# ScalarE takes over one search round of one of VectorE's tiles in three groups of the second step

## The reference

```python
def _adj_from_feats(Xa, W1, W2, W3):
    logits = (Xa @ W1) @ W2 @ (Xa @ W3).T
    idx = jnp.argsort(-logits, axis=1)
    csum = jnp.cumsum(softmax(take_along_axis(logits, idx, 1)), axis=1)
    k_i = jnp.sum(csum < 0.9, axis=1) + 1       # how many of the largest make up 0.9 of the mass
    keep = the k_i largest of each row
    return softmax(where(keep, logits, -inf))

for s in range(2):
    A = _adj_from_feats(Xa, W1, W2, W3)
    Xf = Rf @ Xf;  Xb = Rb @ Xb;  Xa = A @ Xa   # Rf, Rb: adj scaled by its row and column sums
    Z = Z + (Xf @ U1[s] + Xb @ U2[s] + Xa @ U3[s])
```

## Time and profile before

| | |
|---|---|
| median of 3 runs | 3602.8 us (3601.22 to 3603.57) |
| the profiled execution's own time | 3600.57 us |
| its span, first to last instruction | 3598.8 us |
| VectorE, ScalarE, TensorE busy | 95%, 85%, 80% of the span |
| step 1, group 0 begins on VectorE | at 1587.8 us of the span |
| step 1, VectorE takes over role 1 | at 3008.9 us |

### The profile page before, as it was taken

One profiled execution on the slowest core, in us unless ns is written; L12 is line 12 of the kernel. 1 busy time (PEld: TensorE's weight loads), 2 busy tenths in 40 slices (PEclk: granted clock), 3 DMA queues, 4 the chain that ended last, 5 costly groups with the idle time before them and its releaser, 6 DMA issues. The chain is left out here.

```text
span 3598.8 us, 40441 instructions
## 1 busy us (share of the span) xinstructions
PE 2864.5 (80%) x13536; PEld 2020.1 (56%) x13536; DVE 3434.2 (95%) x4607; ACT 3074.2 (85%) x4185; POOL 467.9 (13%) x483
## 2 busy tenths in 40 slices
PE   6568787878778787646888888879797973789998
PEld 5456566666657576422454454536353552657787
DVE  7999999999999999969999999999999998788997
ACT  6999999999999999759999999999999994455443
POOL 3000000000000000000000000000000000546676
PEclk9679898999889898878998999989898996999999
DMA  2112221223121221054221112111121210578996
GB/s 97 58 67 75 71 91 64 88 69 100 55 98 59 89 71 51 22 161 100 48 50 33 47 41 55 31 50 41 42 47 40 52 18 21 163 198 236 252 266 175
DMA packets 224256, 305.43 MB, mean 85 GB/s; under 512 B 81328, under 2 KB 160624, under 8 KB 220656
## 3 DMA queue, kind: packets, MB, share of 16 engines
q1 hardware_dynamic: 187648, 223.01, 21.5%
q10 hardware_dynamic: 21744, 62.79, 5.0%
q0 software_dynamic: 14656, 17.04, 3.3%
HBM read 232.80 MB, written 59.77 MB: 81 GB/s over the span
## 5 line engine op out<-in xcount | busy, mean ns | idle before, releaser
L738 DVE SCALAR_TENSOR_TENSOR s_dump<-s_rows,s_mid 128x3328 bf16<-128x3328 f32 x551 | 2027.1, 3679 | 1.6 <-issue 0.6
L691 ACT ACTIVATE s_adump<-s_rows,s_mid 128x3327 int8<-128x3327 f32 x295 | 906.0, 3071 | 9.5
L697 ACT ACTIVATE s_adump<-s_rows,s_mid 128x3327 int8<-128x3327 f32 x295 | 902.4, 3059 | 0.0
L952 PE MATMUL bank<-x,s_slab 128*128 128x512 f32 x1352 | 630.5, 609 | 0.0
L952 PEld LDWEIGHTS bank<-x,s_slab 128*128 128x128 f32 x1352 | 264.6, 197 | 277.7 <-issue 265.7
L929 PE MATMUL bank<-kh,qs 128*128 128x512 f16 (+1 forms) x364 | 144.7, 398 | 345.5 <-DVE s_rows L717 324.9
L996 PE MATMUL bank<-hb,s_wT 128*128 128x256 f32 x1352 | 353.4, 406 | 66.5 <-ACT s_wT L570 66.1
L996 PE MATMUL bank<-xab,last_wT 128*128 128x256 f32 x1300 | 337.3, 404 | 50.3 <-ACT last_wT L570 50.2
L952 PE MATMUL bank<-hb,s_slab 128*128 128x257 f32 x1352 | 351.7, 401 | 0.0
L985 PE MATMUL bank<-ident,s_rows 128*128 128x128 f32 x1222 | 206.4, 296 | 153.9 <-DVE s_rows L793 153.0
L996 PEld LDWEIGHTS bank<-hb,s_wT 128*128 128x128 f32 x1352 | 258.8, 202 | 115.2 <-ACT s_wT L570 51.5
(11 more groups left out here) (217 smaller groups left out, 5127.0 us busy)
## 6 DMA issues: line engine op xcount, KB each, us to landing
s_slab<-adjT_dram SPq DMA_DIRECT2D x104, 448.0 KB, 3.7
s_slab<-adjT_dram SPq DMA_DIRECT2D x104, 384.0 KB, 3.6
e_adj<-adjR_dram ACTq DMA_DIRECT2D x23, 1664.0 KB, 7.5
strip<-adjR_dram SPq DMA_DIRECT2D x52, 448.0 KB, 3.5
strip<-adjR_dram SPq DMA_DIRECT2D x52, 384.0 KB, 3.2
e_ring<-sc_d SPq DMA_DIRECT2D x72, 256.0 KB, 3.7
sc_d<-e_stage SPq DMA_DIRECT2D x60, 256.0 KB, 2.6
su_d<-s_su_out ACTq DMA_DIRECT2D x26, 256.0 KB, 2.0
```

Source lines behind the costliest of these rows:

```text
L691: nc.scalar.activation(adump[:], row(g, r), ACT.Sign, bias=st(mid, g, 2), accum_out=cnt[:]).then_inc(S["a_eval"], 1)
L697: nc.scalar.activation(adump[:], row(g, r), ACT.Abs, bias=st(mid, g, 2), accum_out=gap[:]).then_inc(S["a_eval"], 1)
L738: nc.vector.scalar_tensor_tensor(out=dump[:], in0=wide_row(g, r), scalar=st(mid, g, r), in1=wide_row(g, r), op0=ALU.is_le, op1=ALU.mult, a ...
L952: ins = nc.tensor.matmul(acc, slab[:, i % NSLAB, j - PIECES[p], :], s_op[:, j, 0:SN], start=False, stop=(j == NT - 1))
```

## The change

In step 1, for the groups in `HANDED` = (2, 4, 6), ScalarE does the first round (number 0) of role 0, a tile of VectorE's, after its own 19 rounds of the group before, and leaves the new `mid` where VectorE reads it. It takes `begin` for it too, with its own scale, and the last factor -1 turns the sign of ScalarE's `mid` into VectorE's. VectorE leaves out that round's `evaluate`, `judge` and `move` and half of `begin`, and at its round 1 of role 0 waits for ScalarE's semaphore `a_mid`. The counts of all semaphores are changed to suit (`passes`, `handed_to`, `opened`).

For this `sides`, `above` and the two passes are written as functions `signs`, `spread`, `distances`, `settle`. In all of ScalarE's rounds, of both steps, the instruction that computes `mean` moves: it stood before the second pass, behind `fac`, and now stands between `sgn` and the new `mid`.

```diff
+    HANDED = (2, 4, 6) if s == 1 else ()
+
+    def handed_to(g):
+        return sum(h <= g for h in HANDED)
+
+    def passes(g, it, r):
+        return BISECT * g + it - (handed_to(g if it else g - 1) if r == 0 else 0)
...
-            def begin(g, r):
+            def begin(n, g, r, own):
...
-            def sides(g, it):
+            def signs(g, r, own):
+                nc.scalar.activation(adump[:], row(g, r), ACT.Sign, bias=st(mid, g, own), accum_out=cnt[:]).then_inc(S["a_eval"], 1)
+
+            def distances(g, r, own, n):
+                act.wait_ge(S["a_eval"], 2 * n + 1)
+                nc.scalar.activation(over[:], cnt[:], ACT.Identity, scale=st(mid, g, own), bias=st(target, g, own)).then_inc(S["a_over"], 1)
+                nc.scalar.activation(adump[:], row(g, r), ACT.Abs, bias=st(mid, g, own), accum_out=gap[:]).then_inc(S["a_eval"], 1)
+
+            def spread(g, it, own, last):
                 up, down = rate(it)
-                last = -1.0 if it + 1 == BISECT else 1.0
-                nc.scalar.activation(fac[:], st(mid, g, 2), ACT.Copy, scale=last * (down - up) / 2).then_inc(S["a_fac"], 1)
-                nc.scalar.activation(mean[:], st(mid, g, 2), ACT.Copy, scale=last * (down + up) / 2).then_inc(S["a_fac"], 1)
...
+                nc.scalar.activation(fac[:], st(mid, g, own), ACT.Copy, scale=last * (down - up) / 2).then_inc(S["a_fac"], 1)
...
                 nc.scalar.activation(sgn[:], gap[:], ACT.Sign, scale=-1.0, bias=over[:]).then_inc(S["a_sgn"], 1)
+                nc.scalar.activation(mean[:], st(mid, g, own), ACT.Copy, scale=last * (down + up) / 2).then_inc(S["a_fac"], 1)
                 act.wait_ge(S["a_sgn"], n + 1)
                 act.wait_ge(S["a_fac"], 2 * n + 2)
-                nc.scalar.activation(st(mid, g, 2), sgn[:], ACT.Identity, scale=fac[:], bias=mean[:]).then_inc(S["a_mid"], 1)
+                nc.scalar.activation(st(mid, g, own), sgn[:], ACT.Identity, scale=fac[:], bias=mean[:]).then_inc(S["a_mid"], 1)
...
-                    settle(g, n)
+                    settle(g, it, 2, n, last)
+                if g + 1 in HANDED:
+                    n = BISECT * (g + 1) + handed_to(g)
+                    begin(g + 1 + handed_to(g), g + 1, 0, 0)
+                    signs(g + 1, 0, 0)
+                    spread(g + 1, 0, 0, -1.0)
+                    distances(g + 1, 0, 0, n)
+                    settle(g + 1, 0, 0, n, -1.0)
...
             def evaluate(g, it, r):
-                n = BISECT * g + it
-                if it == 0:
-                    dve.wait_ge(begun[r], 2 * (g + 1))
+                if r == 0 and g in HANDED and it == 1:
+                    dve.wait_ge(begun[0], opened(g, 0))
+                    dve.wait_ge(S["a_mid"], BISECT * g + handed_to(g))
+                elif it == 0:
+                    dve.wait_ge(begun[r], opened(g, r))
                 else:
-                    dve.wait_ge(mid_ready[r], n)
-                if n + r >= 1:
-                    dve.wait_ge(mass_done[1 - r], n + r)
+                    dve.wait_ge(mid_ready[r], passes(g, it, r))
+                other = passes(g, it + r, 1 - r)
+                if other >= 1:
+                    dve.wait_ge(mass_done[1 - r], other)
...
-                        evaluate(g, it, r)
-                        if it + r >= 1:
+                        first = 1 if g in HANDED else 0
+                        if 2 * it + r >= first:
+                            evaluate(g, it, r)
+                        if 2 * it + r > first:
                             move(g, it + r - 1, 1 - r)
                         between(g, 2 * it + r)
-                        judge(g, it, r)
+                        if 2 * it + r >= first:
+                            judge(g, it, r)
```

More of the change, by code:

```diff
@@ L538, in exponent, with settle @@
                                      accum_out=st(Z, g, r)).then_inc(S["exp_done"], 1)
-            def begin(g, r):
+            def begin(n, g, r, own):
                 act.wait_ge(S["exp_done"], LOADS.index((g, r)) + 1)
-                nc.scalar.activation(st(target, g, 2), st(Z, g, r), ACT.Copy, scale=2.0 * P_NUC - 1.0).then_inc(S["a_begun"], 1)
-                nc.scalar.activation(st(mid, g, 2), st(Z, g, r), ACT.Copy, scale=-LEAST * 2.0 ** LOG_STEP).then_inc(S["a_begun"], 1)
-                act.wait_ge(S["a_begun"], 2 * (g + 1))
-            def sides(g, it):
-                up, down = rate(it)
-                last = -1.0 if it + 1 == BISECT else 1.0
-                nc.scalar.activation(fac[:], st(mid, g, 2), ACT.Copy, scale=last * (down - up) / 2).then_inc(S["a_fac"], 1)
-                nc.scalar.activation(mean[:], st(mid, g, 2), ACT.Copy, scale=last * (down + up) / 2).then_inc(S["a_fac"], 1)
[L552 to L556, removed]
+                nc.scalar.activation(st(target, g, own), st(Z, g, r), ACT.Copy, scale=2.0 * P_NUC - 1.0).then_inc(S["a_begun"], 1)
+                nc.scalar.activation(st(mid, g, own), st(Z, g, r), ACT.Copy, scale=-LEAST * 2.0 ** LOG_STEP).then_inc(S["a_begun"], 1)
+                act.wait_ge(S["a_begun"], 2 * (n + 1))
+            def signs(g, r, own):
[5 more added lines that the diff above has]
+            def spread(g, it, own, last):
+                up, down = rate(it)
+                nc.scalar.activation(fac[:], st(mid, g, own), ACT.Copy, scale=last * (down - up) / 2).then_inc(S["a_fac"], 1)
+            def settle(g, it, own, n, last):
+                up, down = rate(it)
                 act.wait_ge(S["a_over"], n + 1)
@@ L687, in _ @@
                 r, rounds = (1, FIRST_PART) if g == LAST else (2, BISECT)
-                begin(g, r)
+                begin(g + handed_to(g), g, r, 2)
                 for it in range(rounds):
-                    n = BISECT * g + it
-                    nc.scalar.activation(adump[:], row(g, r), ACT.Sign, bias=st(mid, g, 2), accum_out=cnt[:]).then_inc(S["a_eval"], 1)
-                    sides(g, it)
+                    n = BISECT * g + it + handed_to(g)
+                    last = -1.0 if it + 1 == BISECT else 1.0
+                    signs(g, r, 2)
+                    spread(g, it, 2, last)
                     for b in beats(g, 2 * it):
                         fill(g, b)
-                    above(g, n)
-                    act.wait_ge(S["a_eval"], 2 * n + 1)
-                    nc.scalar.activation(adump[:], row(g, r), ACT.Abs, bias=st(mid, g, 2), accum_out=gap[:]).then_inc(S["a_eval"], 1)
+                    distances(g, r, 2, n)
                     for b in beats(g, 2 * it + 1):
                         fill(g, b)
-                    settle(g, n)
+                    settle(g, it, 2, n, last)
[6 more added lines that the diff above has]
+                    settle(g + 1, 0, 0, n, -1.0)
             for b in range(2 * FIRST_PART + NGRP + 4, 2 * BISECT):
@@ L753, in alone @@
             def alone(it):
-                n = BISECT * LAST + it
                 if it == 0:
-                    dve.wait_ge(begun[0], 2 * (LAST + 1))
-                    dve.wait_ge(mass_done[1], n)
+                    dve.wait_ge(begun[0], opened(LAST, 0))
+                    dve.wait_ge(mass_done[1], passes(LAST, 0, 1))
                 else:
-                    dve.wait_ge(mid_ready[0], n)
+                    dve.wait_ge(mid_ready[0], passes(LAST, it, 0))
                 nc.vector.scalar_tensor_tensor(out=dump[:], in0=wide_row(LAST, 0), scalar=st(mid, LAST, 0), in1=wide_row(LAST, 0),
@@ L774, in go_on @@
                     dve.wait_ge(begun[1], 2 * LAST + 1)
-                    dve.wait_ge(mass_done[0], BISECT * TRIPLES)
+                    dve.wait_ge(mass_done[0], passes(LAST, BISECT, 0))
                 dve.wait_ge(mid_ready[1], n + 1)
@@ L791, in cut @@
                 else:
-                    dve.wait_ge(mid_ready[r], BISECT * (g + 1))
+                    dve.wait_ge(mid_ready[r], passes(g, BISECT, r))
                 nc.vector.scalar_tensor_tensor(out=wide_row(g, r), in0=wide_row(g, r), scalar=st(mid, g, r), in1=wide_row(g, r),
```

16 lines of the change are left out of this document (8 added, 8 removed).

## The result

The changed kernel takes 3625.2 us (median of 4 runs) against 3602.0 us of the kernel before (4 runs, those shown ahead among them): ratio 1.0067, 95% interval 1.0056 to 1.0079, so 23 us slower. The profiled execution has a span of 3623.8 us.

The account below looks back on a forecast made before the run. ScalarE's group start, TensorE's gapless stretch and VectorE's eleventh take were taken as the bound. Delays of 8.6, 18.0 and 25.9 us in groups 2, 4 and 6, plus 0.1 from step 0, gave 3602.8 + 26.0 = 3628.8 us; range 3612 to 3636.

Parts of the forecast that it names:

- The chain: Inside a group: ScalarE's start, some 80 us of TensorE without a gap, VectorE's eleventh take, then VectorE's own work.
- the takes of groups 2, 4 and 6: VectorE's waits for TensorE's logits: some 38 us of new waits in these groups and not elsewhere.
- The price of a handed round: Each round added to ScalarE ahead of groups 2, 4 and 6: 7.94 us, three times, 23.8 us.
- The moved `mean`: In ScalarE's rounds: nothing with a bank between passes, +0.09 us in the others, 0.7 us a group (bounds 0 and 1.7).
- The delays: Lateness per group against the kernel before, passed from ScalarE's starts to VectorE's eleventh takes, +26.0 us at the end.
- VectorE's eleventh takes: VectorE's eleventh `take` of logits in a group; room 0.0 us in groups 2 and 4, 1.0 in 3, 1.5 in 6.
- ScalarE's waits: For TensorE's transposes, group 2 to the take-over: 25.2 us before, to stay above 20 us.
- TensorE's solid stretch too: TensorE's gapless work after ScalarE's group start, 80.7 of 80.7 us busy in group 2, starts 8.6 us late there.
- the first wait of group 8: ScalarE's 4.3 us wait for VectorE's cut, which was forecast 2.8 us nearer, so the wait shrinks by that.
- The second rival (the waits fill up): ScalarE's waits absorb the added work as TensorE gets ahead: about 0, 3603 us; half filled, +13; chance 0.10.
- VectorE as the bound: Rival: VectorE, busy 95%, sets the time and the handed rounds are free: -12.1 us, 3590.7 us; chance 0.03.
- The take-over as the place of the loss: Rival: takes don't hold VectorE, only ScalarE's end does, where VectorE takes over: +20.6 us, 3623 us; chance 0.12.

Follow-up runs that it names:

- e3: Kernel before plus ScalarE's three extra rounds, written to an unread scratch, and the moved `mean`; VectorE keeps all its own rounds: 3626.1 us against 3601.9.
- e4: Kernel before with VectorE's first role 0 round left out in groups 2, 4 and 6, done by nobody; ScalarE as before: 3599.1 us against 3601.9.
- e6: The whole change with TensorE's sweeps respread in groups 1 to 7 of step 1 (9 halves, not 14, in beats 3 to 21): 3609.7 us against 3602.1.
- e7: Handed rounds in groups 2, 4 and 6, `mean` in its old place, sweeps spread as in e6: 3603.0 us against 3602.1 for the kernel before.
- e2: The change with `mean` put back in its old place, so only the handed rounds: 3619.5 us against 3601.9 for the kernel before.
- e12: Only groups 3 and 6 handed, `mean` in its old place, sweeps as in e6, logits one beat earlier in those groups: 3594.9 us against 3601.7 before.
- e1: The change without handed rounds, so only `mean` moved: 3604.9 us against 3601.9 for the kernel before.

## Why the prediction was right, point by point

Forecast were 3628.8 us and +26.0, measured 3625.2 us and +23.2.

**The chain.** Right, and shown from four sides: the lateness of ScalarE alone gives the whole loss (e3), less work on VectorE alone gives next to nothing (e4), TensorE's work in between carries it (e6 and e7 against the change and e2), and where both are loosened, with two handed rounds, the saving comes out (e12). The waits stand where they were said to: at the takes of groups 2, 4 and 6, 33.2 us in place of "some 38".

**The price of a handed round.** Right: 7.94 us forecast, and ScalarE's timeline has its `begin` for group 2's handed round at 1921.87 and the next at 1929.82, 7.95 us.

**The moved `mean`.** Mis-sized: it was forecast at half of what it cost. A round with nothing between the passes, after the change:

```profile
2412.61 3.07 ACT L554 ACTIVATE s_adump<-last_row,s_mid 128x3327 int8<-128x3327 f32 x1
2415.59 0.19 ACT L554 ACTIVATION_READ_ACCUMULATOR s_adump<-last_row,s_mid 128x1 f32 x1
2415.68 0.19 ACT L563 ACTIVATE s_fac<-s_mid 128x1 f32<-128x1 f32 x1
2415.80 0.39 ACT L558 ACTIVATE s_over<-s_cnt,s_target,s_mid 128x1 f32<-128x1 f32 x1
2416.10 3.06 ACT L559 ACTIVATE s_adump<-last_row,s_mid 128x3327 int8<-128x3327 f32 x1
2419.06 0.19 ACT L559 ACTIVATION_READ_ACCUMULATOR s_adump<-last_row,s_mid 128x1 f32 x1
2419.34 0.29 ACT L569 ACTIVATE s_sgn<-s_gap,s_over 128x1 f32<-128x1 f32 x1
2419.54 0.19 ACT L570 ACTIVATE s_mean<-s_mid 128x1 f32<-128x1 f32 x1
2419.82 0.39 ACT L573 ACTIVATE s_mid<-s_sgn,s_mean,s_fac 128x1 f32<-128x1 f32 x1
2420.24 3.07 ACT L554 ACTIVATE s_adump<-last_row,s_mid 128x3327 int8<-128x3327 f32 x1
```

The new `mid` starts 0.48 us after `sgn`, not 0.42: it follows the start of `mean` by 0.28 us, not by its 0.19 and 0.03. In front, `over` comes 0.21 us after the reading out, not 0.28 as in the earlier trace rows, so there something was gained after all. The round is 7.63 us long against 7.52: +0.11, with 0.09 forecast. In rounds with a bank between the passes the same two distances give +0.06 (0.15 behind less 0.09 in front) where I had 0. With eight rounds of the first kind and eleven of the second that makes 1.5 us a group, an estimate from these distances, twice the forecast's 0.7 and near its upper bound of 1.7.

**The delays.** ScalarE's starts were forecast 8.6, 17.9 and 27.3 us late and VectorE's eleventh takes 8.6, 18.0 and 25.9. Measured: 8.9, 18.1 and 25.8 (before, group 6 began at 2586.36 us), and 8.1, 16.5 and 23.1. ScalarE's starts are so near in part by luck: in groups 2 to 5 `mean` cost some 3 us more than forecast, and ScalarE's waits, taken as unchanged, fell from 15.0 to 9.8 us. And a single trace isn't finer than 1 us here: from the start of group 0 to the end of group 1, where ScalarE has the same list in e1 and in the change, it takes 329.8 us in e1 and 330.9 in the change. What was mis-sized for VectorE is "TensorE's solid stretch too": it was taken as unchanged and was 1 to 2 us shorter. The stretches from TensorE's last such wait for ScalarE to the eleventh logits in groups 2, 4 and 6, before (to be read with the earlier trace rows):

```profile
1941.20:2022.00 80.80, 80.80 (x303) 50.89 (x304) 80.32 (x103) 77.47 (x105) 3.41 (x4) 0.98 0.18 43
2273.30:2355.80 82.50, 82.50 (x307) 52.02 (x308) 82.33 (x106) 76.08 (x101) 3.44 (x4) 0.98 0.17 40
2606.70:2687.80 81.10, 80.91 (x303) 50.70 (x304) 81.10 (x104) 77.51 (x105) 3.41 (x4) 0.98 0.17 43
```

and after the change:

```profile
1950.20:2030.10 79.90, 79.62 (x303) 50.18 (x304) 68.87 (x88) 77.35 (x105) 3.40 (x4) 1.00 0.19 43
2291.50:2372.30 80.80, 80.80 (x307) 50.86 (x308) 68.75 (x88) 75.81 (x102) 3.44 (x4) 1.00 0.19 41
2632.50:2712.40 79.90, 79.60 (x303) 50.16 (x304) 69.97 (x88) 77.35 (x105) 3.41 (x4) 1.00 0.18 43
```

The same 303 and 307 matmuls take 0.9, 1.7 and 1.2 us less, at a granted clock of 1.00 in place of 0.98. Before, the clock fell from its higher level to the lower one (0.50, 1.2 GHz) once more just behind the start of the stretch; in the change it didn't. The same place of group 2, before and after:

```profile
1943.00:1945.00 2.00, 2.00 (x4) 1.00 (x4) 1.85 (x8) 2.00 (x4) 0.00 (x0) 0.50 0.00 0
```

```profile
1952.00:1954.00 2.00, 2.00 (x6) 0.95 (x5) 2.00 (x5) 2.00 (x4) 0.00 (x0) 1.00 0.00 0
```

The longer wait at the group's start (14.5 us in place of 5.6) suggests itself as the cause, but other traces don't bear it out. In e3 TensorE waits 13.4 and 13.9 us at the start of groups 2 and 6, and both stretches stand at 0.98; in e1 it waits 5.4 us at the start of group 2, and the stretch stands at 1.00:

```profile
1950.10:2030.90 80.80, 80.79 (x303) 50.90 (x304) 72.98 (x92) 77.32 (x104) 3.41 (x4) 0.98 0.18 43
...
2633.90:2714.70 80.80, 80.80 (x303) 51.31 (x304) 72.26 (x92) 77.35 (x105) 3.41 (x4) 0.98 0.18 43
```

```profile
1941.30:2021.60 80.30, 80.02 (x305) 50.53 (x306) 80.15 (x101) 77.74 (x106) 3.41 (x4) 1.00 0.19 43
```

What makes the clock fall that second time stays open, and so these 1 to 2 us a group are not shown to be an effect of the change. Of the 2.8 us by which group 6's eleventh take came sooner than forecast, 1.5 are ScalarE's sooner start and 1.2 group 6's own shorter stretch. e12's order of the logits wasn't tried with all three groups and the moved `mean`; by e6 hardly more than the loss could come back there.

**ScalarE's waits.** I said that they would stay above 20 us; they fell from 25.2 to 13.0, hardly above the half (12.6) below which the prediction called itself wrong. Of the 12 us, 4.3 are the first wait of group 8, which was forecast to shrink by 2.8 and is gone; 3.8 are as much as the three stretches got shorter; the rest is of the size of `mean`'s 0.06 in the rounds with a bank. This split is worked out from sizes and wasn't tried. The second rival (the waits fill up) thus came true in its effect in part, but not in its mechanism: TensorE didn't get ahead, it waits 14.5, 12.6 and 12.3 us for ScalarE at the start of groups 2, 4 and 6. Together with group 6's shorter stretch it puts the take-over 22.7 us later and not 25.9.

**The other rivals.** VectorE as the bound is refuted by e4. The take-over as the place of the loss isn't seen: ScalarE is ready 4.3 us before it. A slower TensorE had the wrong sign. The end, 25.0 us later in the profiled span, is the take-over's 22.7 and 2.3 us of the untouched part behind it.

## What to carry to other kernels

A share of 95% busy doesn't make an engine the bound: ask at which instruction its own list last touched another engine's, and how much room each such touch has; here touches with no room made 12 us less work worth 2.7. Work that is moved to an engine with waits can cost most of its length (in e2 17.7 us for three rounds of 7.84) if those waits lie behind the point at which that engine releases a third one; either that third one's list must have room before the next touch, or its order must be loosened there. And the engine that takes the work must have the room in its own list: here two rounds fitted, three with the moved `mean` didn't. To see which, do one half of the move at a time: only the added work, and only the removed.

## What the hardware showed that I had not expected

A small ScalarE instruction that waits on a semaphore for what the one just before it wrote starts 0.28 us after that one's start (`mean` at 2419.54, `mid` at 2419.82), where two that don't depend on each other start 0.09 us apart (the two in the earlier trace rows); the producer's own record lasts only 0.19 us. And the granted clock of TensorE fell back to its lower level once more after it had risen at a group's start, in some groups of some kernels and not in others, worth 1 to 2 us in 80 (0.98 against 1.00 of the clock); by e1 and e3 the length of the idle time ahead doesn't decide it.
